# Attention in single slots: the weighing of a slot behind the next slot's scores

## The chip, the cores and the metric

The kernel runs on one core of a Trainium2 chip. Its time is that of the whole program on the device, in microseconds; the median of several executions is compared. The profiled execution is one more execution with the hardware profiler on; its span is the time from its first to its last instruction.

## What is computed

One transformer layer for two batches of 1024 tokens of width 256. Cross attention comes first: queries from the normalised x, keys and values from 64 context rows and the normalised x together (1088 keys), eight heads of 64, L2-normalised queries and keys, a mask on the context keys, softmax, output projection and a layer norm. Behind it stands a mixture of experts (one shared, 16 routed, two for each token).

```
q = l2norm(q) * q_scale;  k = l2norm(k) * k_scale
sim = einsum('bhid,bhjd->bhij', q, k) * 8
sim = where(full_mask, sim, max_neg)
attn = softmax(sim, axis=-1)
out = einsum('bhij,bhjd->bhid', attn, v)
x = x + layer_norm(out @ Wo, ln_o_w, ln_o_b)
x = x + shared_expert(ln(x)) + gated sum of two of 16 routed experts(ln(x))
```

The scores run over 1024 queries and 1088 keys for each head and batch (the kernel has nine key tiles of 128, the last one for the context, masked in what it doesn't fill). Everything is in float32, the products of keys and queries in two parts, high and low.

## The kernel before, in words

Each engine has its own program (a block each for SyncE, GpSimd, TensorE, ScalarE, VectorE), and what one waits for is written by hand with semaphores. An engine takes its program strictly in the order written.

The attention works on eight pairs of heads (PAIRS, stage_b(i)). A pair has two chunks of 512 queries; a chunk has nine key tiles of 128 (TK). One chunk with one key tile is a slot, so a pair has 18 slots (SLOTS). The work of a slot:

- **Scores** (score_slot, L812). Four pairs of matmuls, one of each pair for either head, on two halves of the rows of the array (64*128 in the profile): high by high, high by low, low by high (L828), and the negative row maximum (L837). Slots alternate between banks 0, 1 and 2, 3, so slot n waits for the exponentials of slot n-2.
- **Exponentials** (L1174, ScalarE), two of 128x512, into prob, a ring of six slots (PROBS).
- **Weighing** (weigh, L840, matmuls of L854): the two heads stand on two halves of the columns (128*64), with the probabilities streamed past the values. It adds up in bank 7 over nine slots and waits for the slot's exponentials. Each head's matmul appears as two instructions in the profile.
- **Row sums**: GpSimd adds the probabilities of six slots (L634, L639), VectorE the last three (add_tail, L1415, into tail), and GpSimd adds tail (L645). total(m) (L858, L863) spreads the sum of chunk m by a matmul with ones. keep_sum and keep_o (L1176, L1183, ScalarE) copy sum and output, a DMA chain inverts the sum on 128 partitions (invert_sums), and divide (L1425) multiplies.

Beside pair i the next pair is prepared: five **turns** (turn_heads, L756, transposes of L766) whose results ScalarE rounds (high part, round_heads) and VectorE splits (low part, split_heads, L1365), and 17 **rounds** (piece_round, L769; matmuls of L782, also on two halves of the rows) with coarse scores, of which VectorE takes the row maximum (reduce_round, L1375, two for each round, 128x512). The last round is the masked one (L788, L793). The maxima are negated (negate), transposed (turn_neg, L802) and spread (keep_neg, L1393). In pair 0 half of its own second chunk's rounds are still to be done as well (FIRST_ROUNDS).

Turns, rounds, sums and maxima share a **ring** of three banks (bank 4 to 6; RING, ring_put, ring_order). ring_at fixes their order. A round takes two banks (ring_two, L745) and waits until the earlier holders of both are released, for a round by VectorE's reduce. So of two rounds behind one another the second needs the first bank of the first.

The slots are run in **phases** of three (BATCH, PHASES): for phase f TensorE runs its turns, then three times a slot's scores with rounds between them (TURN_AT, ROUNDS), and then the weighing of the three slots of the phase before; total follows in phases 0 and 3, and in the last pair an output projection (project_o, L897, L908) in phases 4 and 5. ScalarE and VectorE have the same loops, with their own steps at phase boundaries. Behind the last pair VectorE runs stage_c(t) for the layer norms of the projected tiles, stage_c(0), add_tail(15), stage_c(1), divide(15), stage_c(2), and TensorE the hidden units of the shared expert (hidden, L992, L997), where the second waits for y_used of stage_c(2).

Of the kernel before, what the change touches and what calls it, by code (L numbers as in the profile page):

```python
# [58 lines left out]
BATCH = 3  # L59
PHASES = TK // BATCH  # L60
RING = 3
SLOTS = CH * TK
PROBS = 2 * BATCH
# [12 lines left out]
def build(nc, x, ctx, mask, ln_x_w, ln_x_b, ln_l_w, ln_l_b, wq, wkv, q_scale, k_scale, wo,  # L76
# [154 lines left out]
    summed, tail_ready, o_ready = sem("summed"), sem("tail_ready"), sem("o_ready")  # L231
# [32 lines left out]
    def slot_loop(eng, body):  # L264
# [6 lines left out]
        for s in range(NS // 4 * 4, NS + 1):  # L271
# [5 lines left out]
    TURN_AT = {0: (K_LEFT, Q_LEFT), 1: (K_RIGHT, K_CTX, Q_RIGHT)}  # L277
    ROUNDS = {1: ((), (0,), (1,), (2,)), 2: ((3,), (4,), (5,), (6,)), 3: ((), (), (7,), (8,)),
              4: ((9,), (10,), (11,), (12,)), 5: ((13,), (14,), (15,), (16,))}
# [3 lines left out]
    LATE_NEG = 2  # L283
    FIRST_TURNS = {0: ((0, Q_RIGHT),), 1: ((1, K_LEFT), (1, Q_LEFT)), 2: ((1, K_RIGHT), (1, K_CTX), (1, Q_RIGHT))}
    FIRST_ROUNDS = {0: (((0, 8),), ((0, 9),), ((0, 10),), ((0, 11),)),
                    1: (((0, 12),), ((0, 13),), ((0, 14),), ((0, 15),)),
                    2: (((0, LATE_MASKED),), (), ((1, 0),), ((1, 1),)),
# [3 lines left out]

    def phase_turns(i, f):

        if i == 0:
            return FIRST_TURNS.get(f, ())
        return [(i + 1, g) for g in TURN_AT.get(f, ())] if i + 1 < PAIRS else []

    def phase_rounds(i, f):

        if i == 0:  # L300
            return FIRST_ROUNDS[f]
        if i + 1 == PAIRS:
            return [()] * (BATCH + 1)
        return [[(i + 1, r) for r in place] for place in ROUNDS.get(f, ((),) * (BATCH + 1))]

# [30 lines left out]
    for i in range(PAIRS):  # L336
        ring_put("neg", i)
        for f in range(CH * PHASES):
            for turn in phase_turns(i, f):
                ring_put("turn", *turn)  # L340
            for a, place in enumerate(phase_rounds(i, f)):
                if i == 0 and f == LATE_NEG and a == 1:
                    ring_put("late_neg", 0)
                for j, r in place:
                    ring_rounds(j, (r,))
            if f == PHASES:
                ring_put("sum", 2 * i)
            if f == 0 and i:
                ring_put("sum", 2 * i - 1)
# [337 lines left out]
    def _(pe):  # L687
# [152 lines left out]
        def weigh(n):  # L840
# [7 lines left out]
            if kt == 0:  # L848
                if m == NCH - 1:
                    pe.wait_ge(o_ready, m)  # L850
                else:
                    wait(pe, o_kept, m)
# [59 lines left out]
        def stage_b(i):  # L912

            more = i + 1 < PAIRS
            turn_neg(i)
            for f in range(CH * PHASES):
                for turn in phase_turns(i, f):
                    turn_heads(*turn)
                places = phase_rounds(i, f)
                for one in places[0]:  # L920
                    piece_round(*one)
                for a in range(BATCH):
                    score_slot(i, BATCH * f + a)
                    if i == 0 and f == LATE_NEG and a == 0:
                        turn_late_neg()
                    for one in places[a + 1]:
                        piece_round(*one)
                for a in range(BATCH):
                    n = SLOTS * i + BATCH * (f - 1) + a
                    if n >= 0:  # L930
                        weigh(n)
# [804 lines left out]
```

## Time and profile before

| | before |
|---|---|
| median of 3 executions | 861.41 us (859.89 to 861.41) |
| profiled execution | 860.57 us |
| its span | 858.8 us, 12948 instructions |
| TensorE matmuls, share of the span | 805.9 us, 94% |
| VectorE | 486.3 us, 57% |
| ScalarE | 342.3 us, 40% |
| GpSimd | 327.9 us, 38% |
| mean granted clock of TensorE | 0.989 |

The profile's page gives busy times, the span in 40 slices of 21.5 us with a digit for the busy share in tenths, the costliest groups of instructions by line, and the chain of work that ended last. The attention lies at about 115 to 500 us. The start of a matmul is what was recorded; its end is modelled, so durations of following matmuls overlap, and the distance from start to start is the better measure. "PEld" is TensorE's loading of weights, "64*128" and "128*64" name the part of the array that an instruction uses.

### The profile page before, as it was taken

What the parts mean: (1) busy time and instruction counts of PE and PEld (TensorE: products, weight loads), DVE (VectorE), ACT (ScalarE), POOL (GpSimd) and SP (SyncE); (2) the same over time, 40 slices, a digit from 0 to 9 for tenths busy, and PEclk for the clock granted to TensorE, in tenths of its full rate; (3) what the DMA queues carried; (4) which work ended last, traced back from release to release, by engine and by line L of the source; (5) the groups of instructions that cost most, each with busy time, mean ns of one, the idle gap of its engine ahead of it and who ended that gap; (6) DMA issues with size and microseconds to landing.
All of it is one profiled execution on the core that took longest, in us unless ns stands there. A gap on an engine that the chain in (4) does not pass through costs nothing.

```text
span 858.8 us, 12948 instructions
## 1 busy us (share of the span) xinstructions
PE 805.9 (94%) x4329; PEld 490.4 (57%) x4330; DVE 486.3 (57%) x904; ACT 342.3 (40%) x652; POOL 327.9 (38%) x250
## 2 busy tenths in 40 slices
PE   4999988999999999999999999999769999999996
PEld 2444444545554454545554547655437999998554
DVE  2888777776776777676762576655013343432433
ACT  2555364555655565555655311121002333333101
POOL 2100034466665656565658743204720000001670
PEclk9999999999999999999999999999879999999999
DMA  3014700000000000000020010862410222232440
GB/s 111 26 37 155 243 1 1 14 13 13 13 14 2 13 13 14 15 12 14 14 75 13 25 61 26 285 217 96 162 62 31 93 91 92 92 92 68 123 140 24
DMA packets 55252, 55.98 MB, mean 65 GB/s; under 512 B 11810, under 2 KB 50340, under 8 KB 55204
## 3 DMA queue, kind: packets, MB, share of 16 engines
q1 hardware_dynamic: 50980, 46.96, 17.6%
q0 software_dynamic: 3072, 8.39, 3.0%
q8 instruction: 28, 0.46, 0.2%
q10 hardware_dynamic: 1152, 0.00, 0.1%
q14 instruction: 20, 0.16, 0.1%
HBM read 36.60 MB, written 18.67 MB: 64 GB/s over the span
## 4 chain that ended last, share of the span: by engine, by line
PE 80%; issue 5%; POOL 4%; DVE 4%; ACT 3%; another core or an unknown queue 2%; DVEq 1%; DMA 1%; ACTq 0%; POOLq 0%
PE bank L854 12%; PE bank L705 10%; PE bank L997 10%; PE bank L828 10%; PE bank L1062 10%; PE bank L1012 6%; PE bank L782 5%; PE bank L1071 5%; PE bank L837 3%; POOL acc L639 2%; ACT prob L1174 2%; PE bank L908 2%; PE bank L766 2%; PE bank L863 1%
## 5 line engine op out<-in xcount | busy, mean ns | idle before, releaser
L1174 ACT ACTIVATE prob<-bank,zero 128x512 f32<-128x512 f32 x256 | 158.8, 692 | 103.9 <-PE bank L837 98.4
L1375 DVE TENSOR_REDUCE mx<-bank 128x1 f32<-128x512 f32 x256 | 164.4, 686 | 54.5 <-PE bank L782 54.1
L639 POOL TENSOR_TENSOR acc<-acc,prob 128x1024 f32<-128x1024 f32 x64 | 152.5, 2383 | 26.4 <-ACT prob L1174 19.3
L854 PE MATMUL bank<-prob,vn 128*64 128x512 f32 x576 | 134.2, 601 | 0.6 <-DVE on L1440 0.6
L997 PE MATMUL bank<-xfT,w12s 128*128 128x512 f32 x256 | 116.2, 599 | 1.8 <-DVE yn L1523 1.1
L681 POOL DMA_INDIRECT slot_result<-slot_results,posi x32 | 30.6, 958 | 176.5 <-DMA slot_results<-yo 162.8
L1062 PE MATMUL bank<-xsT,w_slot 128*128 128x128 f32 x752 | 91.9, 275 | 1.0 <-ACT xsT L1264 1.0
L1062 PEld LDWEIGHTS bank<-xsT,w_slot 128*128 128x128 f32 x752 | 89.2, 191 | 6.0 <-ACT xsT L1264 1.6
L1254 ACT ACTIVATE sil<-bank 128x512 f32<-128x512 f32 x32 | 18.9, 597 | 155.8 <-PE bank L997 102.4
L1012 PE MATMUL bank<-w3s,gsh 128*128 128x256 f32 x256 | 64.7, 397 | 16.8 <-DVE gsh L1507 10.5
L997 PEld LDWEIGHTS bank<-xfT,w12s 128*128 128x128 f32 x256 | 49.2, 193 | 53.1 <-issue 49.7
L645 POOL TENSOR_TENSOR acc<-acc,tail 128x1024 f32<-128x1024 f32 x16 | 38.1, 2381 | 107.5 <-DVE tail L1423 107.5
L854 PEld LDWEIGHTS bank<-prob,vn 128*64 128x64 f32 x576 | 37.2, 136 | 68.0 <-issue 45.1
L828 PE MATMUL bank<-q_hi,k_hi 64*128 64x512 f32 x288 | 63.1, 432 | 8.1 <-ACT prob L1174 8.0
L1012 PEld LDWEIGHTS bank<-w3s,gsh 128*128 128x128 f32 x256 | 50.0, 199 | 34.4 <-issue 16.2
L782 PE MATMUL bank<-k_hi,q_hi 64*128 64x512 f32 x256 | 62.1, 481 | 5.7 <-DVE mx L1375 2.0
L1507 DVE TENSOR_TENSOR gsh<-sil,bank 128x512 f32<-128x512 f32 x32 | 21.8, 685 | 74.1 <-ACT sil L1254 41.7
L837 PE MATMUL bank<-neg_max,ones_r 64*128 64x512 f32 x288 | 57.4, 392 | 0.0
L828 PE MATMUL bank<-q_hi,k_lo 64*128 64x512 f32 x288 | 57.2, 390 | 0.0
L828 PE MATMUL bank<-q_lo,k_hi 64*128 64x512 f32 x288 | 57.1, 390 | 0.0
L1673 DVE TENSOR_TENSOR rgT<-sil,bank 128x256 f32<-128x256 f32 x47 | 19.8, 422 | 65.2 <-ACT sil L1269 65.2
L705 PE MATMUL bank<-wqkv,xT 128*128 128x512 f32 x112 | 52.3, 616 | 3.2 <-ACT xT L1105 3.2
(161 smaller groups left out, 1069.1 us busy)
## 6 DMA issues: line engine op xcount, KB each, us to landing
w12r<-in_L_ffn_routed_w SPq DMA_DIRECT2D x32, 256.0 KB
slot_rows<-zrow SPq DMA_DIRECT2D x47, 128.0 KB, 1.9
xsl<-slot_rows SPq DMA_DIRECT2D x47, 128.0 KB, 2.0
slot_results<-yo SPq DMA_DIRECT2D x47, 128.0 KB, 1.7
w3r<-in_L_ffn_routed_w SPq DMA_DIRECT2D x16, 256.0 KB
rec<-row_sum_reciprocals SPq DMA_DIRECT2D x28, 128.0 KB, 2.9
xin<-in_x SPq DMA_DIRECT2D x16, 128.0 KB, 2.1
w12s<-in_L_ffn_shared_w SPq DMA_DIRECT2D x2, 1024.0 KB, 6.7
```

Source lines behind the costliest of these rows:

```text
L639: g.tensor_tensor(acc[:, m % 2, :, :], acc[:, m % 2, :, :], prob[:, (n + kt) % PROBS, :, :], ALU.add).then_inc(summed, 1)
L705: last = mm_(dst[:, :], xT_of(n, c)[:, k, :], wqkv[:, k, j * INNER:(j + 1) * INNER], start=(k == 0), stop=(k == DK - 1))
L782: mm_(two[h][:, :], q_hi[p][rows, t * P:(t + 1) * P], k_hi[p][rows, c * QC:(c + 1) * QC], start=True, stop=True).then_inc(ring_made, 1)
L828: mm_(two[h][:, :], lhs[rows, keys], rhs[rows, queries], start=(lhs is k_hi[p] and rhs is q_hi[p]), stop=False)
L837: mm_(two[h][:, :], ones_r[rows, :], neg_max[rows, queries], start=False, stop=True)\
L854: last = mm_(bank[O_BANK][rows, :], vn[:, kt, b, (2 * j + h) * DH:(2 * j + h + 1) * DH], prob[:, n % PROBS, h, :], start=(kt == 0), stop=( ...
L997: last = mm_(bank[2 * (u % 2) + w][:, :], w12s[:, k, w, u * P:(u + 1) * P], xfT[:, k, bass.ds(g * GR, GR)], start=(k == 0), stop=(k == DK ...
L1012: last = mm_(bank[4 + j // 2][:, (j % 2) * D:(j % 2 + 1) * D], gsh[:, u % 2, j * P:(j + 1) * P], w3s[:, u, :], start=(u == 0 and j % 2 == ...
L1062: last = mm_(bank[2 + p][:, j * P:(j + 1) * P], w_slot[:, p, k, j * P:(j + 1) * P], xsT[:, p, k, :], start=(k == 0), stop=(k == DK - 1))
L1071: last = mm_(bank[6 + p][:, 0:D], rgT[:, p, k * P:(k + 1) * P], w3r[:, e, k, :], start=(k == 0), stop=(k == HID // P - 1))
L1174: a(prob[:, n % PROBS, h, :], bank[2 * (n % 2) + h][:, :], ACT.Exp, bias=bias).then_inc(probs_ready, 1)
L1375: v.tensor_reduce(mx[:, h, t, c:c + 1], ring_bank(u)[:, :], AX.X, ALU.max).then_inc(ring_used, 1)
```

## The change

Phases are gone; everything is laid to single slots. For slot s of a pair TensorE now runs: the slot's turns, its scores, its rounds, and then the weighing of the slot before. total of the chunk before stands behind slot 2 and 11 of a pair (SUM_AT), projections of the last pair behind slots 14 and 16 (PROJECT_AT). New tables say which turns and rounds go with which slot; some slots have two rounds. ring_at follows the same order.

ScalarE keeps the sum in slots 3 and 12 (KEEP_SUM_AT), without the wait for an earlier division, which keep_o takes over; it copies the output (keep_o) behind the exponentials of slots 0 and 9, now also for the first chunk of the last pair.

VectorE's tail add is split: begin_tail adds the first two of three in slot 8 or 17, end_tail the third in the slot that follows, with a semaphore (tail_begun) in the place of a drain. The reciprocal of the sums is in slots 5 and 14, the division in slots 8 and 17 (slot 13 for the first chunk of the last pair), negate in slot 16. With that begin_tail(15) stands ahead of stage_c(0), and end_tail(15) behind it.

```diff
...
 NCH = PAIRS * CH
-BATCH = 3
-PHASES = TK // BATCH
 RING = 3
 SLOTS = CH * TK
-PROBS = 2 * BATCH
+PROBS = 6
 TURNS = 5
...
     scores_made, probs_ready, pv_done = sem("scores_made"), sem("probs_ready"), sem("pv_done")
-    summed, tail_ready, o_ready = sem("summed"), sem("tail_ready"), sem("o_ready")
+    summed, tail_begun, tail_ready, o_ready = sem("summed"), sem("tail_begun"), sem("tail_ready"), sem("o_ready")
     sum_kept, o_kept, sum_spread = sem("sum_kept"), sem("o_kept"), sem("sum_spread")
...
     K_LEFT, Q_LEFT, K_RIGHT, K_CTX, Q_RIGHT = range(TURNS)
-    TURN_AT = {0: (K_LEFT, Q_LEFT), 1: (K_RIGHT, K_CTX, Q_RIGHT)}
-    ROUNDS = {1: ((), (0,), (1,), (2,)), 2: ((3,), (4,), (5,), (6,)), 3: ((), (), (7,), (8,)),
-              4: ((9,), (10,), (11,), (12,)), 5: ((13,), (14,), (15,), (16,))}
+    TURNS_AT = {0: (K_LEFT, Q_LEFT), 2: (K_RIGHT,), 3: (K_CTX,), 4: (Q_RIGHT,)}
+    ROUNDS_AT = {1: (0,), 2: (2,), 3: (4,), 4: (6,), 5: (1,), 6: (3, 5), 7: (7,), 9: (8,), 10: (9,), 11: (10, 11),
+                 12: (MASKED_ROUND,), 13: (12,), 14: (13,), 15: (14,), 16: (15,)}
 
...
     LATE_MASKED = MASKED_ROUND + 1
-    LATE_NEG = 2
-    FIRST_TURNS = {0: ((0, Q_RIGHT),), 1: ((1, K_LEFT), (1, Q_LEFT)), 2: ((1, K_RIGHT), (1, K_CTX), (1, Q_RIGHT))}
-    FIRST_ROUNDS = {0: (((0, 8),), ((0, 9),), ((0, 10),), ((0, 11),)),
-                    1: (((0, 12),), ((0, 13),), ((0, 14),), ((0, 15),)),
-                    2: (((0, LATE_MASKED),), (), ((1, 0),), ((1, 1),)),
-                    3: (((1, 2), (1, 3)), ((1, 4),), ((1, 5),), ((1, 6),)),
-                    4: (((1, 7), (1, 8)), ((1, 9),), ((1, 10),), ((1, 11),)),
-                    5: (((1, 12), (1, 13)), ((1, 14),), ((1, 15),), ((1, 16),))}
-
-    def phase_turns(i, f):
+    LATE_NEG = 8
+    FIRST_TURNS_AT = {0: ((0, Q_RIGHT),), 1: ((1, K_LEFT),), 2: ((1, Q_LEFT),), 5: ((1, K_RIGHT),), 6: ((1, K_CTX),),
+                      9: ((1, Q_RIGHT),)}
+    FIRST_ROUNDS_AT = {1: ((0, 8), (0, 9)), 2: ((0, 10),), 3: ((0, 11), (0, 12)), 4: ((0, 13), (1, 0)),
+                       5: ((0, 14), (0, 15)), 6: ((0, LATE_MASKED),), 7: ((1, 2), (1, 4)), 8: ((1, 6),),
+                       9: ((1, 1),), 10: ((1, 3), (1, 5)), 11: ((1, 7),), 12: ((1, 8), (1, 9)), 13: ((1, 10),),
+                       14: ((1, 11), (1, 12)), 15: ((1, MASKED_ROUND), (1, 13)), 16: ((1, 14), (1, 15))}
+
+    SUM_AT, KEEP_SUM_AT, INVERT_AT, DIVIDE_AT, TAIL_AT = 2, 3, 5, TK - 1, TK - 1
+    PROJECT_AT = {SLOTS - 4: 0, SLOTS - 2: 1}
+
+    def slot_turns(i, s):
 
         if i == 0:
-            return FIRST_TURNS.get(f, ())
-        return [(i + 1, g) for g in TURN_AT.get(f, ())] if i + 1 < PAIRS else []
-
-    def phase_rounds(i, f):
+            return FIRST_TURNS_AT.get(s, ())
+        return [(i + 1, g) for g in TURNS_AT.get(s, ())] if i + 1 < PAIRS else []
+
+    def slot_rounds(i, s):
 
         if i == 0:
-            return FIRST_ROUNDS[f]
-        if i + 1 == PAIRS:
-            return [()] * (BATCH + 1)
-        return [[(i + 1, r) for r in place] for place in ROUNDS.get(f, ((),) * (BATCH + 1))]
+            return FIRST_ROUNDS_AT.get(s, ())
+        return [(i + 1, r) for r in ROUNDS_AT.get(s, ())] if i + 1 < PAIRS else []
+
+    def chunk_before(i, s):
+
+        return CH * i + s // TK - 1
 
...
         ring_put("neg", i)
-        for f in range(CH * PHASES):
-            for turn in phase_turns(i, f):
+        for s in range(SLOTS):
+            if i == 0 and s == LATE_NEG:
+                ring_put("late_neg", 0)
+            for turn in slot_turns(i, s):
                 ring_put("turn", *turn)
-            for a, place in enumerate(phase_rounds(i, f)):
-                if i == 0 and f == LATE_NEG and a == 1:
-                    ring_put("late_neg", 0)
-                for j, r in place:
-                    ring_rounds(j, (r,))
-            if f == PHASES:
-                ring_put("sum", 2 * i)
-            if f == 0 and i:
-                ring_put("sum", 2 * i - 1)
+            for j, r in slot_rounds(i, s):
+                ring_rounds(j, (r,))
+            if s % TK == SUM_AT and chunk_before(i, s) >= 0:
+                ring_put("sum", chunk_before(i, s))
     ring_put("sum", NCH - 1)
...
             if kt == 0:
-                if m == NCH - 1:
-                    pe.wait_ge(o_ready, m)
-                else:
-                    wait(pe, o_kept, m)
+                wait(pe, o_kept, m)
             for h, rows in enumerate((LOW, HIGH)):
...
 
-            more = i + 1 < PAIRS
             turn_neg(i)
-            for f in range(CH * PHASES):
-                for turn in phase_turns(i, f):
+            for s in range(SLOTS):
+                n = SLOTS * i + s
+                if i == 0 and s == LATE_NEG:
+                    turn_late_neg()
+                for turn in slot_turns(i, s):
                     turn_heads(*turn)
-                places = phase_rounds(i, f)
-                for one in places[0]:
+                score_slot(i, s)
+                for one in slot_rounds(i, s):
                     piece_round(*one)
-                for a in range(BATCH):
-                    score_slot(i, BATCH * f + a)
-                    if i == 0 and f == LATE_NEG and a == 0:
-                        turn_late_neg()
-                    for one in places[a + 1]:
-                        piece_round(*one)
-                for a in range(BATCH):
-                    n = SLOTS * i + BATCH * (f - 1) + a
-                    if n >= 0:
-                        weigh(n)
-                if f == PHASES:
-                    total(2 * i)
-                if f == 0 and i:
-                    total(2 * i - 1)
-                if not more and f > PHASES:
-                    project_o(f - PHASES - 1)
+                if n:
+                    weigh(n - 1)
+                if s % TK == SUM_AT and chunk_before(i, s) >= 0:
+                    total(chunk_before(i, s))
+                if i + 1 == PAIRS and s in PROJECT_AT:
+                    project_o(PROJECT_AT[s])
 
...
             stage_b(i)
-        for a in range(BATCH):
-            weigh(SLOTS * PAIRS - BATCH + a)
+        weigh(SLOTS * PAIRS - 1)
         project_o(EARLY)
...
             act.wait_ge(ring_made, u + 1)
+            a(rec[:, m % 2, :], ring_bank(u)[:, :], ACT.Copy).then_inc(sum_kept, 1)
+
+        def keep_o(m):
+
+            act.wait_ge(pv_done, TK * (m + 1))
             wait(act, o_ready, m - 1)
-            a(rec[:, m % 2, :], ring_bank(u)[:, :], ACT.Copy).then_inc(sum_kept, 1)
-
-        def keep_o(m):
-
-            act.wait_ge(pv_done, TK * (m + 1))
             a(o_raw[:, m % 2, :], bank[O_BANK][:, :], ACT.Copy).then_inc(o_kept, 1)
...
             for s in range(SLOTS):
-                f, a_ = divmod(s, BATCH)
-                m = 2 * i - 1 if f == 1 else 2 * i if f == PHASES + 1 and i + 1 < PAIRS else -1
-                if a_ == 0 and m >= 0:
+                m = chunk_before(i, s)
+                if s % TK == KEEP_SUM_AT and 0 <= m < NCH - 2:
                     keep_sum(m)
-                if a_ == 0:
-                    for turn in phase_turns(i, f):
-                        round_heads(*turn)
+                for turn in slot_turns(i, s):
+                    round_heads(*turn)
                 exponentials(i, s)
-                if a_ == 0 and m >= 0:
+                if s % TK == 0 and m >= 0:
                     keep_o(m)
...
 
-        def add_tail(m):
+        def begin_tail(m):
 
...
             wait(dve, summed, ADDS * m)
-            v.tensor_tensor(tail[:, :, :], prob[:, n % PROBS, :, :], prob[:, (n + 1) % PROBS, :, :], ALU.add)
-            v.drain()
+            v.tensor_tensor(tail[:, :, :], prob[:, n % PROBS, :, :], prob[:, (n + 1) % PROBS, :, :],
+                            ALU.add).then_inc(tail_begun, 1)
+
+        def end_tail(m):
+
+            n = TK * m + ADDS
+            dve.wait_ge(tail_begun, m + 1)
             dve.wait_ge(probs_ready, 2 * (n + LAST))
...
                 v.drain()
+            else:
+                dve.wait_ge(rec_loaded, 32 * (m + 1))
+            if m == NCH - 1:
                 dve.wait_ge(pv_done, TK * (m + 1))
...
             else:
-                dve.wait_ge(rec_loaded, 32 * (m + 1))
                 dve.wait_ge(o_kept, m + 1)
...
             more = i + 1 < PAIRS
-            for f in range(CH * PHASES):
-                if f == 0:
+            for s in range(SLOTS):
+                m = chunk_before(i, s)
+                if s == 0:
                     keep_neg(i)
-                    if i:
-                        add_tail(2 * i - 1)
-                if f == PHASES:
-                    add_tail(2 * i)
-                for turn in phase_turns(i, f):
+                if i == 0 and s == LATE_NEG:
+                    keep_late_neg()
+                for turn in slot_turns(i, s):
                     split_heads(*turn)
-                for a, place in enumerate(phase_rounds(i, f)):
-                    if i == 0 and f == LATE_NEG and a == 1:
+                if s % TK == 0 and m >= 0:
+                    end_tail(m)
+                if s % TK == TAIL_AT:
+                    begin_tail(m + 1)
+                for one in slot_rounds(i, s):
+                    reduce_round(*one)
+                    if one == (0, LATE_MASKED):
                         negate(0, HALF, TQ)
-                        keep_late_neg()
-                    for one in place:
-                        reduce_round(*one)
-                if f == PHASES and not more:
-                    divide(2 * i)
-                for m, first in ((2 * i - 1, 0), (2 * i, PHASES)):
-                    if f == first + 1 and 0 <= m < NCH - 2:
-                        invert_sums(m)
-                    if f == first + 2 and 0 <= m < NCH - 2:
-                        divide(m)
-            if more:
-                negate(i + 1)
+                if s == SLOTS - 2 and more:
+                    negate(i + 1)
+                if s % TK == INVERT_AT and 0 <= m < NCH - 2:
+                    invert_sums(m)
+                if s % TK == DIVIDE_AT and 0 <= m < NCH - 2:
+                    divide(m)
+                if s == SLOTS - 5 and not more:
+                    divide(m)
 
...
         stage_c(0)
-        add_tail(NCH - 1)
+        end_tail(NCH - 1)
         stage_c(1)
...
         v.drain()
```

## Rows read from the trace of the kernel before

**Rows 1.** The page: busy tenths of TensorE in 40 slices.

```profile
PE   4999988999999999999999999999769999999996
```

**Rows 2.** Windows of pairs: length, busy us by engine, granted clock, DMA.

```profile
117.00:169.00 52.00, 46.27 (x309) 25.55 (x310) 40.68 (x67) 26.54 (x44) 26.05 (x11) 1.00 0.03 6
...
307.10:353.20 46.10, 45.31 (x295) 23.74 (x293) 32.56 (x51) 27.09 (x45) 28.44 (x12) 1.00 0.06 13
```

**Rows 3.** Timeline of TensorE: start, us, line, operation.

```profile
136.65 0.40 PE L782 MATMUL bank<-k_hi,q_hi 64*128 64x512 f32 x2
136.88 0.39 PE L828 MATMUL bank<-q_hi,k_hi 64*128 64x512 f32 x2
```

**Rows 4.** Timeline of TensorE, first phases of a middle pair.

```profile
309.92 0.41 PE L837 MATMUL bank<-neg_max,ones_r 64*128 64x512 f32 x2
310.84 0.50 PE L828 MATMUL bank<-q_hi,k_hi 64*128 64x512 f32 x2 [0.51 <-ACT prob L1174]
...
311.64 0.39 PE L837 MATMUL bank<-neg_max,ones_r 64*128 64x512 f32 x2
311.96 2.79 PE L854 MATMUL bank<-prob,vn 128*64 128x512 f32 x12
314.59 1.03 PE L863 MATMUL bank<-acc,ones_r 128*64 128x512 f32 x4
```

**Rows 5.** The page's costliest groups: busy us, mean ns, idle before.

```profile
L1174 ACT ACTIVATE prob<-bank,zero 128x512 f32<-128x512 f32 x256 | 158.8, 692 | 103.9 <-PE bank L837 98.4
L1375 DVE TENSOR_REDUCE mx<-bank 128x1 f32<-128x512 f32 x256 | 164.4, 686 | 54.5 <-PE bank L782 54.1
```

**Rows 6.** Timeline of weight loads: a weighing group's second pair.

```profile
312.44 0.14 PEld L854 LDWEIGHTS bank<-prob,vn 128*64 128x64 f32 x2 [0.29 <-issue]
```

**Rows 7.** Timeline of TensorE, a phase with four rounds.

```profile
320.58 0.50 PE L782 MATMUL bank<-k_hi,q_hi 64*128 64x512 f32 x2
321.02 2.80 PE L854 MATMUL bank<-prob,vn 128*64 128x512 f32 x12
323.74 0.50 PE L782 MATMUL bank<-k_hi,q_hi 64*128 64x512 f32 x2
324.08 0.39 PE L828 MATMUL bank<-q_hi,k_hi 64*128 64x512 f32 x2
```

**Rows 8.** Timeline of TensorE, pair 0: two rounds behind one another.

```profile
159.11 0.50 PE L782 MATMUL bank<-k_hi,q_hi 64*128 64x512 f32 x2
160.39 0.50 PE L782 MATMUL bank<-k_hi,q_hi 64*128 64x512 f32 x2 [0.78 <-DVE mx L1375]
```

**Rows 9.** Waits over the span: us in total, times, longest.

```profile
PE bank L828 <- ACT prob L1174: 8.0, 18, 0.6
...
PEld bank L782 <- DVE mx L1375: 25.0, 75, 1.6
...
PEld bank L854 <- ACT prob L1174: 22.6, 73, 1.0
...
PEld bank L828 <- ACT prob L1174: 16.3, 19, 1.0
```

**Rows 10.** TensorE's waits from 115 to 169 us, the same columns.

```profile
PE bank L782 <- DVE mx L1375: 2.0, 2, 1.3
...
PE bank L809 <- DVE zneg L1388: 0.4, 1, 0.4
```

**Rows 11.** Timelines of VectorE and TensorE, last pair to hidden units.

```profile
445.67 0.50 PE L828 MATMUL bank<-q_hi,k_hi 64*128 64x512 f32 x2
...
484.44 0.76 DVE L1298 BATCH_NORM_STATS2 st<-bank 128x6 f32<-128x256 f32 x2 [6.70 <-PE bank L908]
...
490.59 1.22 DVE L1420 TENSOR_TENSOR tail<-prob 128x1024 f32<-128x1024 f32 x1
...
494.51 0.76 DVE L1298 BATCH_NORM_STATS2 st<-bank 128x6 f32<-128x256 f32 x2 [0.49 <-PE bank L908]
...
508.76 3.70 PE L997 MATMUL bank<-xfT,w12s 128*128 128x512 f32 x8 [1.07 <-DVE yn L1523]
```

More of the change, by code:

```diff
@@ L1179, in keep_sum @@
             act.wait_ge(ring_made, u + 1)
-            wait(act, o_ready, m - 1)
             a(rec[:, m % 2, :], ring_bank(u)[:, :], ACT.Copy).then_inc(sum_kept, 1)
@@ L1185, in keep_o @@
             act.wait_ge(pv_done, TK * (m + 1))
+            wait(act, o_ready, m - 1)
             a(o_raw[:, m % 2, :], bank[O_BANK][:, :], ACT.Copy).then_inc(o_kept, 1)
```

## The prediction, before the change was run

> **What bounds the kernel now.** I read the page's slices first: up to about 500 us nearly every digit of TensorE is 9 [rows 1]. The attention is eight pairs of heads. In a middle pair of 46.1 us TensorE is busy 45.3 us, VectorE 32.6, ScalarE 27.1 and GpSimd 28.4, at a granted clock of 1.00 [rows 2]. So TensorE bounds it, and a change pays there only if it shortens the distance from one matmul's start to the next. A busy share doesn't show that, since durations overlap, so I work with distances of starts in the timeline. A "pair" of matmuls below is two that run side by side and count as one start.
>
> In steady order a pair with two row halves (scores, rounds) follows its predecessor by 0.23 us (136.65 to 136.88) [rows 3]. Weighing works in two column halves: 0.43 us a pair (314.59 - 311.96 is 2.63 us for six) [rows 4]. A slot is four score pairs, 0.92 us, and two weighing pairs, 0.86 us. ScalarE needs 2 x 0.69 us for it, and VectorE 2 x 0.69 for a round [rows 5].
>
> **The change part by part.**
>
> *(a) Weighing in groups of one slot.* The number of weighing groups goes from 48 to 143: in each of pairs 0 to 6 twelve more. What one group costs beyond its matmuls: entering it, 0.32 us in place of 0.23 (311.64 to 311.96) [rows 4], 0.09. Its first pair, 0.48 in place of 0.43 (311.96 to 312.44) [rows 4, 6], 0.05. Leaving it for a row-split tile, 2.72 us (321.02 to 323.74) [rows 7] in place of 2.63 [rows 4], 0.09. The first row-split pair behind it, 0.34 us (323.74 to 324.08) [rows 7] in place of 0.23, 0.11, because its weights weren't loaded ahead. Sum 0.34 us. Groups of one slot don't occur before, so the bounds are 0.18 (entering and leaving alone) and 0.34; I take 0.34, as every group of the trace shows all four. 84 x 0.34 = **+28.6 us**. The last pair is treated in (f).
>
> The Trainium skill, TensorEngine Tiling, Key Properties, says that changing the tiling mode drains TensorE; it gives no price. Its page TensorE: Matmul & The Clock Gate, Step-by-step: what each phase is for, has weight loads pulled ahead of running matmuls and a drain of about 128 cycles. An estimate from that page, 128 cycles at 2.4 GHz and two changes a group, is 0.107 us; 84 of those are 9 us and the whole sum would be 872 us. The rows above show more than three times that, so they decide.
>
> *(b) Two rounds behind one another.* A round takes two of three ring banks, so the second of two rounds needs a bank that the first has just filled and VectorE must reduce. The trace has this case with VectorE free: 159.11 to 160.39, 1.28 us in place of 0.23 [rows 8], 1.05 lost, and then 0.11 for a restart with unloaded weights, some 1.15. Before, three such places exist, all in pair 0. Of the new table, ROUNDS_AT has two (slots 6 and 11) for each of pairs 1 to 6, and FIRST_ROUNDS_AT has ten. 22 x 1.15 = **+25.3 us**. Nothing hides it: the weighing that could stands behind both rounds in TensorE's queue. Bounds: 1.05 and 1.15 each if the wait stands, 0 if it doesn't.
>
> *(c) Turns.* Transposes are now in four groups for a pair in place of two, six in place of three in pair 0. Each further group is one more change of tile split, 0.09, with a slower first start of 0.05, some 0.15: 15 x 0.15 = **+2.2 us**. ScalarE and VectorE make the parts one at a time, ahead of the rounds that need them by over 2 us.
>
> *(d) Waits that go, pairs 1 to 6.* After two slots without rounds the third waits for ScalarE: 309.92 to 310.84, 0.92 in place of 0.23, 0.69 [rows 4]. In the fourth phase the same wait, with one round ahead of it, costs 0.44, and each restart 0.11: 1.3 us a pair (over the span 18 such waits, 8.0 us idle [rows 9]). In the new order scores of slot n need the exponentials of n-2, which are ready 1.5 us earlier, and the weighing of n-1 comes 0.8 us behind its exponentials (score done, 2 x 0.69 us, against a weighing, four score pairs and a round). Within a phase rounds come every 1.27 us and VectorE takes 1.3 for one, so the round's weights load late: 0.34 in place of 0.23, or 0.44 in place of 0.32 where a weighing follows (320.58 to 321.02) [rows 7]. That is some 1.7 us a pair. With a slot of 2.3 us VectorE keeps up. Together 3.0 x 6 = **-18.0 us**.
>
> *(e) Pair 0.* TensorE waits six times, 7.1 us ([rows 10] has the first and the last of six), 9 us with the restarts; late rounds give another 1.5. These go, since the scores stand ahead of rounds and turns: **-10.5 us**. For new waits of the same kind, as its slots hold twice the rounds, I put **+1.0 us**, an estimate.
>
> *(f) The last pair and the end.* It has no rounds, so a new slot takes 0.34 + 0.23 + 0.23 between its scores, 0.32 into the weighing, 0.48 within and 0.52 out of it, 2.12 us; TensorE alone would end some 2.7 us sooner. But VectorE's order sets the end. Before, stage_c(0) starts as soon as the first output projection is made (484.44), ends at 490.59, stage_c(1) runs from 494.51, and the second hidden unit starts at 508.76, when VectorE has released its bank [rows 11]. In the new order begin_tail(15) stands ahead of stage_c(0) and waits for the exponentials of slot 16. Measured from the pair's first score (445.67): slot 16 begins at 16 x 2.12 + two totals of 0.86 + one projection of 3.7 + 0.7 for a maximum that comes later, = 40.0; exponentials +2.6; begin_tail 1.3 gives 43.9. Stage_c(0) 6.15, end_tail 1.7, stage_c(1) 8.0, then division and stage_c(2) up to the release 6.2: 65.9 us, before 63.1. **+2.8 us**. The total of chunk 15 waits for GpSimd's last add, but that is off this chain.
>
> Keeping the sum (keep_sum) one slot after its total and o_raw after a chunk's first exponentials: ScalarE has the room (27 of 46 us), o_raw is ready 0.25 us before the first weighing of the next chunk wants the bank. Taken at nothing; what it costs without that cover stands under the rivals. The two DMAs of the sums have two slots for one and three for the other, 4.7 and 7 us, against one landing of 2.9 us (the page's median for rec) and two in a row, 5.8: nothing. On VectorE end_tail waits for the last slot's exponentials ahead of the next round's reduces; that round's banks are wanted again only a slot (2.3 us) later: nothing. If one of these covers goes, the wait costs its length once a chunk, as in R3.
>
> Sum: 28.6 + 25.3 + 2.2 - 18.0 - 10.5 + 1.0 + 2.8 = +31.4 us. The profiled execution took 860.57 us (span 858.8), 0.84 below the median of 861.41. 860.57 + 31.4 = **892 us**. Work behind attention only shifts.
>
> **Rivals.**
> *R1, weights are loaded ahead in short groups*, so that a group costs 0.18 us. 84 x 0.16 = 13.4 less: 879 us. For it: a group of two pairs leaves the queue of loads less to do. Against: every entry in the trace shows the first distance of 0.48.
> *R2, the second round doesn't wait*, because the bank is free by then. 25.3 less: 867 us. Against it is 159.11 to 160.39, with an idle VectorE before it.
> *R3, chunk boundaries get late.* TensorE waits at a chunk's first weighing for o_raw, which has 0.25 us of cover; from there on each microsecond costs 15 at 15 boundaries: with 1 us late, 907 us. Behind that wait stand all later scores, and so ScalarE.
> *R4, faster.* The weight loads of rounds wait 25.0 us for VectorE, those of weighing and scores 22.6 and 16.3 us for ScalarE [rows 9], 63.9 us. If that were lost time, the credit would be 63.9 and not the 28.5 of (d) and (e): 892 - 35.4 = 857 us. It decides from a credit of 60 us. Against it: TensorE itself waits for ScalarE just 8.0 us [rows 9], and a load that waits 0.28 us costs 0.11 us of distance.
>
> **How the numbers follow.** Forecast 0.56 (about 884 to 898, by its own terms: 1 us in each of the pairs' credits either way), R1 0.15, R2 0.07, R3 0.14, R4 0.08, of which 0.06 is faster and 0.02 no change. 0.2% (1.7 us) is about what a measurement of this kernel can tell. The range from 874 to 907 takes in the forecast, R1 and R3's 1 us, and leaves out R2, R4 and a worse R3. Faster 0.06, same 0.02, slower 0.92.
>
> **What would show it.** (a): groups of four weighing matmuls, 0.32 ahead of them and 0.34 behind; if the row-split pair behind is 0.23, R1. (b): 22 distances of about 1.28 between rounds, with VectorE's reduce as the releaser; if absent, R2. (d): no wait of scores for ScalarE in pairs 1 to 6, a middle pair of about 49.9 us in place of 46.1. (e): pair 0 of some 59 us in place of 52. (f): stage_c(0) starts behind begin_tail. A wait of the weighing for L1186's copy would be R3. The forecast is wrong if a middle pair takes less than 48.5 us.

## The result and the profile after

The changed kernel takes 893.59 us (median of four, 892.86 to 896.42), the kernel before 861.07 on the same chip. The ratio is 1.0387, 95% interval 1.0366 to 1.0408. The forecast was 892, from 874 to 907. The profiled execution took 896.42 us, some 3 above the other three, so it is read for where time lies and the medians for how much.

The page of after: busy times, and TensorE's tenths in 40 slices.

```profile
PE 832.0 (93%) x4329; PEld 481.5 (54%) x4330; DVE 483.6 (54%) x904; ACT 349.1 (39%) x653; POOL 327.1 (37%) x250
...
PE   5999988899999999999999979999849999999996
```

TensorE issues the same 4329 matmuls as before and is busy 26 us longer, which only says that starts are further apart. Three windows of after, from one pair's turned maximum to the next's: pair 0, a middle pair, the last pair up to the second hidden unit.

```profile
113.70:176.30 62.60, 53.21 (x316) 25.34 (x315) 41.90 (x68) 28.87 (x46) 26.05 (x11) 0.97 0.02 5
325.00:374.60 49.60, 48.04 (x295) 22.48 (x293) 32.58 (x52) 27.93 (x46) 28.47 (x12) 1.00 0.05 12
474.00:544.20 70.20, 61.36 (x298) 29.07 (x298) 31.16 (x51) 27.00 (x43) 41.66 (x34) 0.95 0.15 45
```

Against [rows 2] the middle pair has grown from 46.1 to 49.6 us. Read in the same way (start of the transposed maximum to the next one), pair 0 went from 53.6 to 62.6, pairs 1 to 6 together from 277.2 to 297.4, the end from 63.3 to 70.5 us. Pair 0 starts 0.9 us earlier. That is -0.9 + 9.0 + 20.2 + 7.2 = 35.5 us of the 35.85 us between the two profiled executions, so hardly anything changes behind the attention.

The timeline of TensorE in slot 6 of a middle pair of after shows both main costs. The last two rows are the next round and the weighing behind it.

```profile
343.20 0.39 PE L836 MATMUL bank<-neg_max,ones_r 64*128 64x512 f32 x2
343.43 0.40 PE L781 MATMUL bank<-k_hi,q_hi 64*128 64x512 f32 x2
344.60 0.50 PE L781 MATMUL bank<-k_hi,q_hi 64*128 64x512 f32 x2 [0.78 <-DVE mx L1360]
345.03 1.08 PE L850 MATMUL bank<-prob,vn 128*64 128x512 f32 x4
346.04 0.50 PE L827 MATMUL bank<-q_hi,k_hi 64*128 64x512 f32 x2
346.38 0.40 PE L827 MATMUL bank<-q_lo,k_hi 64*128 64x512 f32 x2
346.62 0.39 PE L827 MATMUL bank<-q_hi,k_lo 64*128 64x512 f32 x2
...
347.08 0.40 PE L781 MATMUL bank<-k_hi,q_hi 64*128 64x512 f32 x2
347.40 1.08 PE L850 MATMUL bank<-prob,vn 128*64 128x512 f32 x4
```

The first round follows the scores by 0.23 us, and a weighing behind a round that doesn't wait follows by 0.32: the rounds' weights are loaded ahead. Before, they mostly were not, and scores followed a round by 0.33 or 0.34 us. The second round follows by 1.17 us, released by VectorE's reduce, as in [rows 8]. The weighing is a group of four instructions; from its start to the scores are 1.01 us for 0.86 us of work, and the first score pair is followed at 0.34 us, the next at 0.24.

### The profile page after: what moved, and what is told of

It reads as the page before. It is cut to its first block, busy times and chain, and to the rows that moved or that the text cites. A ratio compares the mean times of both kernels' runs of the same rounds, so it can differ in the third digit from the quotient of the medians.

```text
span 894.7 us, 12957 instructions
## 1 busy us (share of the span) xinstructions
PE 832.0 (93%) x4329; PEld 481.5 (54%) x4330; DVE 483.6 (54%) x904; ACT 349.1 (39%) x653; POOL 327.1 (37%) x250
## 4 chain that ended last, share of the span: by engine, by line
PE 84%; issue 4%; POOL 3%; DVE 3%; DMA 2%; another core or an unknown queue 2%; ACT 1%; DVEq 0%; ACTq 0%; POOLq 0%; SPq 0%
PE bank L850 14%; PE bank L827 12%; PE bank L984 12%; PE bank L704 10%; PE bank L1049 9%; PE bank L999 6%; PE bank L1058 4%; PE bank L781 4%; PE bank L836 3%; PE bank L904 2%; PE bank L765 2%; POOL acc L638 2%; DVE mx L1360 2%; PE bank L859 1%
## 5 line engine op out<-in xcount | busy, mean ns | idle before, releaser
L1161 ACT ACTIVATE prob<-bank,zero 128x512 f32<-128x512 f32 x256 | 162.2, 684 | 131.8 <-PE bank L836 131.8
L850 PE MATMUL bank<-prob,vn 128*64 128x512 f32 x576 | 156.0, 620 | 0.4 <-ACT prob L1161 0.4
L984 PE MATMUL bank<-xfT,w12s 128*128 128x512 f32 x256 | 119.0, 612 | 0.8 <-ACT xfT L1214 0.8
L827 PEld LDWEIGHTS bank<-q_hi,k_hi 64*128 64x128 f32 x288 | 26.9, 183 | 95.0 <-ACT prob L1161 74.7
L827 PE MATMUL bank<-q_hi,k_hi 64*128 64x512 f32 x288 | 72.3, 498 | 0.0
L781 PE MATMUL bank<-k_hi,q_hi 64*128 64x512 f32 x256 | 53.8, 416 | 19.0 <-DVE mx L1360 18.0
L836 PE MATMUL bank<-neg_max,ones_r 64*128 64x512 f32 x288 | 56.9, 392 | 1.7 <-DVE neg_max L1378 1.7
L827 PE MATMUL bank<-q_lo,k_hi 64*128 64x512 f32 x288 | 57.2, 392 | 0.0
L827 PE MATMUL bank<-q_hi,k_lo 64*128 64x512 f32 x288 | 56.9, 391 | 0.0
L633 POOL TENSOR_TENSOR acc<-prob 128x1024 f32<-128x1024 f32 x16 | 38.0, 2376 | 47.1 <-ACT prob L1161 47.1
```

The source lines that it names most:

```text
L633: g.tensor_tensor(acc[:, m % 2, :, :], prob[:, n % PROBS, :, :], prob[:, (n + 1) % PROBS, :, :], ALU.add).then_inc(summed, 1)
L781: mm_(two[h][:, :], q_hi[p][rows, t * P:(t + 1) * P], k_hi[p][rows, c * QC:(c + 1) * QC], start=True, stop=True).then_inc(ring_made, 1)
L827: mm_(two[h][:, :], lhs[rows, keys], rhs[rows, queries], start=(lhs is k_hi[p] and rhs is q_hi[p]), stop=False)
L836: mm_(two[h][:, :], ones_r[rows, :], neg_max[rows, queries], start=False, stop=True)\
L850: last = mm_(bank[O_BANK][rows, :], vn[:, kt, b, (2 * j + h) * DH:(2 * j + h + 1) * DH], prob[:, n % PROBS, h, :], start=(kt == 0), stop=( ...
L984: last = mm_(bank[2 * (u % 2) + w][:, :], w12s[:, k, w, u * P:(u + 1) * P], xfT[:, k, bass.ds(g * GR, GR)], start=(k == 0), stop=(k == DK ...
```

## The experiments

The runs lie on three further chips. There the kernel before takes 838.74 us (e1 to e4), 838.48 (e5 to e8) and 838.39 (e9, e10), so their medians can be set beside one another. The changed kernel itself ran on the second of them (e5).

**e5: the changed kernel again.**

> The changed kernel unedited, so that the others can be compared with it on one chip. Before and after should lie 32 us apart (ratio 1.039 by the first comparison, somewhat less on a chip with a shorter total), with a middle pair of 49.6 us whatever the chip.

872.22 us, ratio 1.0404 (1.0387 to 1.0422), 33.7 us over before. The window of the middle pair, on this chip too:

```profile
325.90:375.50 49.60, 48.04 (x295) 22.58 (x293) 32.58 (x52) 27.90 (x46) 28.46 (x12) 1.00 0.04 12
```

So the loss is about the same, 32.5 and 33.7 us, where the totals of the two chips differ by 21 to 23. 872.2 is what e1 to e4 and e8 to e10 are compared with.

**e1: the second round of a slot behind the weighing.**

```diff
-                for one in slot_rounds(i, s):
+                for one in slot_rounds(i, s)[:1]:
                     piece_round(*one)
                 if n:
                     weigh(n - 1)
                 if s % TK == SUM_AT and chunk_before(i, s) >= 0:
                     total(chunk_before(i, s))
+                for one in slot_rounds(i, s)[1:]:
+                    piece_round(*one)
```

The order of the ring is changed in the same way.

> The changed kernel with one edit: where a slot has two rounds, the second stands behind the weighing (and the total, if there is one) in place of directly behind the first. If the wait of a second round for VectorE is what the 22 double slots cost, 22 x 1.05 us go (the distance of 1.18 instead of 0.23 us and 0.10 in front of the weighing), and 1.3 us more at the first of them: about 870 us. If double rounds cost nothing on the path that sets the end, it stays at 893.6 us. If all of the loss comes from the change of tile split, it doesn't move either.

851.96 us, 20.3 below the changed kernel, where 870 in place of 893.6 had been expected, 23.6 below. The middle pair takes 47.8 us with no wait left in it, pair 0 52.9:

```profile
311.00:358.80 47.80, 47.80 (x295) 22.45 (x293) 32.52 (x52) 27.89 (x46) 28.46 (x12) 1.00 0.05 12
```

That is 0.9 us for each double of a middle pair and 9.7 for the ten of pair 0. Double rounds are three fifths of the whole loss, and theories without them fall.

**e6: doubles put into the kernel before.**

```diff
-2: ((3,), (4,), (5,), (6,)), ... 4: ((9,), (10,), (11,), (12,))
+2: ((3,), (4,), (5, 6), ()), ... 4: ((9,), (10,), (11, 12), ())
```

> The kernel before with one edit: in phases 2 and 4 of pairs 1 to 6 the last round stands directly behind the one before (5, 6 and 11, 12), and nothing behind the last scores. 12 doubles. If a second round waits for VectorE wherever it stands, each costs 1.28 - 0.34 = 0.94 us: a middle pair of 46.1 + 1.9 = 48.0 us, 11 us in all, ratio 1.013. If the wait is covered by something else: no change.

849.86 us, 11.4 over before, ratio 1.0137 (1.0120 to 1.0154). The window of a middle pair, and one of the doubles in TensorE's timeline:

```profile
313.20:361.20 48.00, 45.66 (x294) 23.70 (x292) 32.55 (x51) 27.20 (x45) 28.47 (x12) 1.00 0.04 12
```

```profile
332.47 0.50 PE L782 MATMUL bank<-k_hi,q_hi 64*128 64x512 f32 x2
333.75 0.50 PE L782 MATMUL bank<-k_hi,q_hi 64*128 64x512 f32 x2 [0.78 <-DVE mx L1375]
```

The distance is 1.28 us again and the pair takes 48.0 us as expected. The wait has the same 0.78 us in both kernels.

**e7: one more weighing group, in the kernel before.**

```diff
-                for one in places[0]:
-                    piece_round(*one)
+                if not (i and f in (2, 5)):
+                    for one in places[0]:
+                        piece_round(*one)
...
                     if n >= 0:
                         weigh(n)
+                    if a == 0 and i and f in (1, 4):
+                        for one in phase_rounds(i, f + 1)[0]:
+                            piece_round(*one)
```

> The kernel before with one edit: in pairs 1 to 6 the first round of phases 2 and 5 stands between the first and the second slot of the weighing ahead of it. That makes one more weighing group at 12 places and changes nothing else. If a group costs 0.34 us: a middle pair of 46.1 + 0.7 = 46.8 us, 4 us in all. If 0.18 us: 46.5 us, 2 us in all.

842.43 us, 3.95 over before, ratio 1.0048 (1.0031 to 1.0065): 0.33 us for each of twelve groups, 0.22 to 0.45 by the interval. The window of a middle pair, and the divided group in the timeline:

```profile
310.20:356.90 46.70, 45.90 (x295) 23.80 (x293) 32.58 (x51) 26.84 (x45) 28.41 (x12) 1.00 0.04 12
```

```profile
324.12 1.08 PE L854 MATMUL bank<-prob,vn 128*64 128x512 f32 x4
325.13 0.50 PE L782 MATMUL bank<-k_hi,q_hi 64*128 64x512 f32 x2
325.56 1.94 PE L854 MATMUL bank<-prob,vn 128*64 128x512 f32 x8
327.43 0.49 PE L828 MATMUL bank<-q_hi,k_hi 64*128 64x512 f32 x2
327.76 0.40 PE L828 MATMUL bank<-q_lo,k_hi 64*128 64x512 f32 x2
```

Nothing waits here. 1.01 + 0.43 + 1.87 + 0.33 us make 3.64, where a group of three and a round behind it, 2.72 + 0.34, and the 0.23 of the score pair make 3.29: 0.35 more for the same instructions. The lower bound of 0.18, R1, falls: by the interval narrowly, by the distances clearly.

**e2 and e3: weighing in larger groups, the rest as changed.**

```diff
-                if n:
-                    weigh(n - 1)
+                if s % TK in (0, 2, 4, 6, 8):
+                    while weighed < n:
+                        weigh(weighed)
+                        weighed += 1
...
```

e3 has (0, 3, 6) in place of (0, 2, 4, 6, 8).

> The changed kernel with weighing in groups of two slots (behind the scores of key tiles 2, 4, 6, 8 and 0 of a chunk): 79 groups in place of 143, 56 fewer in pairs 0 to 6. If a group costs 0.34 us beyond its matmuls: 19 us less, of which about 4 come back because every second round again follows the one before by 1.27 us and loads its weights late: about 878 us. If a group costs only 0.18 us: 10 us less and 4 back: 887 us. If the weight loads' waits for ScalarE were lost time (74.7 us in 92 of them in the changed kernel), grouping takes away half of them: under 865 us.

> The changed kernel with weighing in groups of three slots, turns, rounds, tails and sums still laid to single slots: 48 groups as before the change. If a group costs 0.34 us: 84 x 0.34 = 28.6 us less in pairs 0 to 6, and the waits for ScalarE and the late rounds of the phases come back (at most 18 us, rather 14, as rounds are spread otherwise): about 879 us, a middle pair of 47.5 us. If a group costs 0.18: 15 less, 14 back: 893 us.

e2: 859.48 us, 12.7 below the changed kernel. A middle pair takes 47.8 us (one of them 48.4), 1.8 less where 2.1 were expected (19 less and 4 back, over seven pairs). It bears out the price of a group, not sharply, as late rounds come with it: with 0.18 us for a group 6 us would have gone in all.

e3 missed: 877.98 us, 5.8 over the changed kernel, with a middle pair of 50.1 us, where 879 had been expected on a scale on which the changed kernel has 893.6, thus 14 to 15 below it. TensorE's waits in pairs 2 to 6 of e3, with the maximum behind them (columns: us in total, times, longest):

```profile
PE bank L781 <- DVE mx L1367: 7.8, 10, 0.8
PE bank L801 <- DVE zneg L1380: 6.6, 6, 1.1
PE bank L859 <- DVE k_lo L1357: 3.1, 5, 0.6
PE bank L827 <- ACT prob L1168: 1.4, 5, 0.3
PE bank L836 <- DVE neg_max L1385: 1.3, 5, 0.5
```

The doubles (first row) were known, and waits of scores for ScalarE (fourth row) had been expected back. The other three rows are new: with groups of three no weighing stands between the last scores and the transposed maximum (L801), or between a turn and the total that needs its bank (L859). The new tables of turns and rounds rely on a weighing in every slot to cover VectorE's steps. These three rows are 2.0 us a pair, of the 2.6 that I was off in a middle pair. That is read from the waits; no run tested it alone. What makes up the rest isn't shown, nor are the some 5 us that lie outside pairs 1 to 6; pair 0 takes 62.0 us there, hardly less than the 62.6 of e5, where some 2 less had been expected.

**e4: begin_tail(15) behind stage_c(0).**

> The changed kernel with begin_tail(15) behind stage_c(0) on VectorE, as before the change. If VectorE's order sets the end of attention, stage_c(0) starts at about 513.5 us in place of 519.4, and the second hidden unit 5 to 7 us earlier: 887 to 889 us. If TensorE sets it, nothing changes: 893.6 us.

868.84 us, 3.4 below the changed kernel; expected were 5 to 7. VectorE's timeline in after, and then in e4:

```profile
518.05 1.23 DVE L1405 TENSOR_TENSOR tail<-prob 128x1024 f32<-128x1024 f32 x1 [9.96 <-ACT prob L1161]
519.43 0.76 DVE L1283 BATCH_NORM_STATS2 st<-bank 128x6 f32<-128x256 f32 x2 [0.16 <-issue]
```

```profile
512.40 0.76 DVE L1283 BATCH_NORM_STATS2 st<-bank 128x6 f32<-128x256 f32 x2 [5.43 <-PE bank L904]
...
515.29 0.88 DVE L1521 SCALAR_TENSOR_TENSOR x<-yn,rs,xres 128x256 f32<-128x256 f32 x2 [0.84 <-POOL rs L577]
```

stage_c(0) starts as early as it was meant to. A part of the gain goes to GpSimd, whose small steps of stage_c(0) stand behind its sums (VectorE waits 0.84 us for it here, 0.25 in after). The second hidden unit starts at 539.2 us, and at 543.5 in e5. So the moved addition accounts for about half of the 7.2 us of the end.

**e8, e9, e10: what the parts add up to.** e8 has the edits of e1, e2 and e4 together.

> The changed kernel with the second round of a slot behind the weighing, weighing in groups of two slots, and begin_tail(15) behind stage_c(0). If the three costs add up: a middle pair of 47.8 (second round moved) less 8 x 0.34, plus some 0.9 for late rounds, 46.0 us; pair 0 at 51 instead of 62.6 us; the end 3 to 5 us earlier. That is 4 to 6 us below the kernel before, ratio 0.994. If the groups cost 0.18, a middle pair of 47.3 and 4 us above the kernel before.

843.45 us, 28.8 below the changed kernel, but 5 over the kernel before (1.0070, 1.0053 to 1.0086), where 4 to 6 under it had been expected: a miss. The middle pair is right, 45.9 against 46.0. Pair 0 takes 58.2 us, not 51: where no weighing is due, the second round still stands directly behind the first. TensorE's waits in pair 0 of e8, and VectorE's wait for GpSimd in its stage_c(0):

```profile
PE bank L783 <- DVE mx L1371: 7.8, 8, 2.3
```

```profile
490.21 0.88 DVE L1532 SCALAR_TENSOR_TENSOR x<-yn,rs,xres 128x256 f32<-128x256 f32 x2 [2.38 <-POOL rs L579]
```

e9 mends these two:

```diff
-                if s % TK in (0, 2, 4, 6, 8):
+                if i == 0 or s % TK in (0, 2, 4, 6, 8):
...
             for kt in range(2, ADDS):
+                if m == NCH - 1 and kt == ADDS - 1:
+                    deviations_c(0)
...
-            if m == NCH - 1:
-                deviations_c(0)
```

> As e8_all_three, with two edits: pair 0 weighs in single slots again (in e8 a second round still followed directly wherever no weighing was due, eight waits of 7.8 us), and GpSimd takes its two small steps of stage_c(0) ahead of its last but one add (in e8 VectorE waited 2.4 us for them). If these two were what was left: pair 0 at 52.9 us in place of 58.1, the end 2 us earlier, 836 us where the kernel before takes 838.5 (ratio 0.997). If pair 0 has another limit: above 841.

836.63 us, with pair 0 at 52.9 us and the end 2.0 us sooner, both as expected. The ratio of 0.9987 (0.9970 to 1.0003) doesn't separate it from the kernel before.

e10 has all of e9 and `TURNS_AT = {0: (K_LEFT, Q_LEFT), 1: (K_RIGHT,), 3: (K_CTX, Q_RIGHT)}`.

> As e9, and the turns of pairs 1 to 6 in slots 0, 1 and 3 in place of 0, 2, 3 and 4, each directly behind a weighing. Two changes of tile split and one group of turns fewer in a pair: if each costs what the others do (0.25 to 0.34 us), a middle pair of 45.4 in place of 45.9 us, 3 us in all, 833 us, ratio 0.994. If the ring's releases are late for the earlier turns, a middle pair of 46 us or more.

834.99 us, ratio 0.9964 (0.9951 to 0.9978): below the kernel before by 0.36%. The 1.6 us between the medians of e9 and e10, where 3 were expected, don't separate the two: twelve executions of e9 lie between 834.1 and 840.9, eight of e10 between 833.6 and 838.4. From one turned maximum to the next, pairs 1 to 6 together take 275.6 us in e9 and 275.4 in e10. Windows of two middle pairs of e10, the usual one and the one with a wait:

```profile
212.20:258.00 45.80, 45.79 (x295) 23.61 (x293) 31.94 (x52) 26.96 (x45) 28.49 (x12) 1.00 0.05 13
...
303.80:350.00 46.20, 45.97 (x295) 23.52 (x293) 32.22 (x52) 26.99 (x45) 28.49 (x12) 1.00 0.05 13
```

So turns next to a weighing gave next to nothing in the attention, not half a microsecond a pair. Why not, I didn't settle.

## Why the prediction was right, and where its terms were off

**(a) Groups, +28.6 us.** Right, mechanism and size. e7 gives 0.33 us for a group where 0.34 was taken. In after, the parts are in the rows of slots 6 and 7: into the weighing 0.32 (347.08 to 347.40), within and out of it 1.01 (345.03 to 346.04, 0.48 and 0.53 in the working), 0.34 behind. In all 78 places of pairs 1 to 6 where scores stand directly behind a weighing, the first pair is followed at 0.33 to 0.35 us. e7 measures the sum alone; how it divides between the change of split and the late weights is read from distances. That groups of one slot pay the same was the choice between the bounds, and it was right.

**(b) Doubles, +25.3 us.** The mechanism is right, the size of an ordinary one a tenth too large. In pairs 1 to 6 all twelve distances are 1.17 or 1.18 us, not 1.28. The 1.28 of [rows 8] came from a first round that itself stood behind a weighing, with weights that had to be loaded; in the new order the first round has them. With the entry into the weighing at 0.43 in place of 0.33, a double costs 1.05 us: 23 us for 22, of which e1 got 20 back. The first double of pair 0 cost 1.5 us more, under (e), so in all the term came out near its 25.3, for another reason than the one given.

**(c) Turns, +2.2 us.** Not seen alone. e10 has one group of turns and two changes of tile split fewer in each of pairs 1 to 6 than e9, and the six pairs together gain 0.2 us.

**(d) Waits that go, -18.0 us.** The middle pair was forecast at 49.9 us and has 49.6, which is what the sum gives with doubles of 1.05 us. TensorE doesn't wait for ScalarE once in pairs 1 to 6. No run took this credit by itself. TensorE's waits in the attention of after, the weight loads' longest entry, and two of those loads in the timeline:

```profile
PE bank L781 <- DVE mx L1360: 18.0, 21, 2.3
PE bank L836 <- DVE neg_max L1378: 1.7, 1, 1.7
PE bank L781 <- DVE mx L1363: 0.8, 1, 0.8
```

```profile
PEld bank L827 <- ACT prob L1161: 74.7, 92, 0.8
```

```profile
342.40 0.19 PEld L827 LDWEIGHTS bank<-q_hi,k_hi 64*128 64x128 f32 x2 [0.81 <-ACT prob L1161]
...
346.04 0.18 PEld L827 LDWEIGHTS bank<-q_hi,k_hi 64*128 64x128 f32 x2 [0.81 <-issue]
```

The first and third row are the 22 doubles, all of them. The next fence is what R4 rested on: weight loads of the scores "wait" 74.7 us for ScalarE where [rows 9] had 16.3, and no matmul of L827 waits at all. Read as lost time it would have pointed the wrong way. Both loads of the timeline start with their matmul, behind a weighing, and are idle for the same 0.81 us, though one is put down to ScalarE and the other to nothing. So it is the weighing that they stand behind, and ScalarE is merely what the profile finds ahead of one of them.

**(e) Pair 0, +6.6 us together.** It was +9.0. The missed part is its first double. TensorE, VectorE and ScalarE in after, and a window around them:

```profile
117.08 0.39 PE L781 MATMUL bank<-k_hi,q_hi 64*128 64x512 f32 x2
119.73 0.51 PE L781 MATMUL bank<-k_hi,q_hi 64*128 64x512 f32 x2 [2.25 <-DVE mx L1360]
...
122.83 0.79 PE L827 MATMUL bank<-q_hi,k_hi 64*128 64x512 f32 x2
123.42 0.62 PE L827 MATMUL bank<-q_lo,k_hi 64*128 64x512 f32 x2
```

```profile
118.33 0.75 DVE L1350 SCALAR_TENSOR_TENSOR k_lo<-bank,qks,k_hi 128x512 fp32r<-128x512 f32 x1 [2.41 <-ACT k_hi L1143]
118.99 2.55 DVE L1360 TENSOR_REDUCE mx<-bank 128x1 f32<-128x512 f32 x4
```

```profile
115.15 1.28 ACT L1161 ACT_TABLE_LOAD   x1
...
117.60 0.69 ACT L1143 ACTIVATE k_hi<-bank,qks 128x512 fp32r<-128x512 f32 x1
```

```profile
118.00:125.00 7.00, 5.27 (x22) 2.53 (x24) 4.19 (x7) 2.59 (x5) 2.36 (x1) 0.76 0.01 2
```

VectorE takes the slot's turn ahead of its rounds, and the turn's high part was late from ScalarE, which makes it behind its first exponentials and the table load ahead of them, so the double took 2.65 us. I had put +1.0 for such things without looking where. Behind that pause the pairs of matmuls at 122.83 are 0.59 us apart in place of 0.34: the granted clock, 0.76 in the mean of the seven microseconds, was at its lower level of 1.2 GHz for about 3 us of them. By that mean it cost some 1.7 us. These two are more than the 2.4 us that were missed; the cheaper ordinary doubles give about 1 us back. Ahead of the pause TensorE had been busy for 17.5 us without a gap.

**(f) The end, +2.8 us.** The mechanism is right, VectorE's begin_tail(15) stands in the way (519.43 above), the size was too small: +7.2. stage_c(0) began 45.5 us behind the pair's first score (473.96) where 43.9 was worked out. Of these 1.6 us, 1.1 are the maximum of the first slot (the row of L836 above): it held the scores up by 1.8 us where 0.7 was taken. VectorE's row ahead of it, its release of the second hidden unit's bank, and the window of the hidden units:

```profile
475.24 0.69 DVE L1432 TENSOR_TENSOR on<-o_raw,rec 128x512 f32<-128x512 f32 x1 [1.58 <-DMA rec<-row_sum_reciprocals]
...
541.47 0.88 DVE L1515 SCALAR_TENSOR_TENSOR yn<-bank,mv,lno 128x256 f32<-128x256 f32 x2
```

```profile
536.00:546.00 10.00, 8.99 (x17) 3.98 (x18) 7.90 (x15) 2.48 (x3) 2.92 (x12) 0.66 0.31 105
```

A division stands ahead of the spread maximum on VectorE and waited 1.58 us for the DMA of the sums, whose cover the prediction had taken as enough. In e5 it waited 0.51, and the end took 68.8 us there. From stage_c(0) to the release (542.35) VectorE took 22.9 us where 22.1 was worked out. The second hidden unit started another 1.8 us later, at 544.2, 6.5 us behind the first, since TensorE, idle 1.8 and 4.2 us before, ran most of the first at 1.2 GHz. I had the chain of VectorE set the start and no price for that.

**Rivals.** R1 fell with e7, R2 with e1 and e6, R4 with the waits above and the result. R3, a late o_raw, didn't occur: no wait of the weighing for the copy stands in the trace. That the sum came so close has luck in it. By stretches of the profiled execution, pairs 1 to 6 were forecast at +22.1 us and took +20.2, pair 0 at +6.6 and took +9.0, the end at +2.8 and took +7.2, and pair 0 began 0.9 us earlier. That makes 35.5 us where 31.4 had been forecast. The median is 2.8 us below this execution, and no trace shows where the other three executions were shorter.

## What to carry to other kernels

Count how often TensorE changes between tile splits before the order is made finer: here each visit to the other split costs 0.34 us beyond its matmuls, so single slots must save more than that in waits each time. e9 shows how far the new order comes once its two costs are reduced: level with the old one. Where a ring has three banks and a step takes two, never put two such steps behind one another; put work of the same engine between them. Here the second round can start 1.17 us behind the first, and in e1 a weighing between them, with its entry, makes it 1.34 us, so the wait is gone. And read waits of weight loads by what they do to the distance between matmul starts, not by their sum.

## What the runs showed of the hardware

- One chip ran the kernel before in 861 us, three others in 838.4 to 838.7. The first has two pauses of TensorE in its trace, 6.3 us with no releaser and 8.1 us for VectorE, between 608 and 636 us, with ScalarE and VectorE idle for 11 and 17 us; the changed kernel has two in the same stretch of work, 10.0 and 4.5 us between 644 and 671 us, and no trace from the other chips does. They are 14.4 of the 22.6 us between the chips. Their cause stays open, as does the rest of the difference.
- After a wait of 2.25 us in pair 0 the granted clock falls to its lower level for a moment, on two chips alike (0.76 over seven microseconds around it):

```profile
119.00:126.00 7.00, 5.42 (x24) 2.76 (x24) 4.39 (x7) 2.83 (x6) 2.35 (x1) 0.76 0.01 2
```

  The row is of e5; e1, which has no such wait, has no such fall in pair 0.
